# Head weights of an expert layer added up transposed in PSUM, with transposed GELUs and thresholds in place

## What is computed

```
xn = rmsnorm(x) * norm_w
q  = (xn @ w_q.T).reshape(b, t, 8 heads, 2, 128)
sim1, sim2 = q[...,0,:] . keys[...,0,:],  q[...,1,:] . keys[...,1,:]    # 32 each per head
s1, i1 = top_k(sim1, 8);  s2, i2 = top_k(sim2, 8)
fs, pk = top_k(s1[:, None] + s2[None, :], 8)          # 8 best of the 1024 experts (i, j), per head
hidden = gelu(xn . expert_down[fi]) * relu(fs)
out    = sum over heads and picks of hidden * expert_up[fi]
```

## Time and profile before

| | |
|---|---|
| median of 3 runs | 1263.45 us (1261.83 to 1265.84) |
| span of the profiled execution, the only time shown of it | 1266.5 us |
| busy, whole span: PE / DVE / ACT / POOL | 885.7 / 988.6 / 570.6 / 256.6 us |
| mean granted clock of PE | 0.839 |
| expert sublayer in the span | about 448 to 641 us, and 1060 to 1252 us |
| in it, 540 to 580 us: PE / DVE / ACT busy | 35.11 / 39.70 / 28.68 us of 40 |

### The profile page before, as it was taken

One profiled execution on the slowest core, in us unless ns is written; L12 is line 12 of the kernel. 1 busy time (PEld: TensorE's weight loads), 2 busy tenths in 40 slices (PEclk: granted clock), 3 DMA queues, 4 the chain that ended last, 5 costly groups with the idle time before them and its releaser, 6 DMA issues. The chain is left out here.

```text
span 1266.5 us, 10862 instructions
## 1 busy us (share of the span) xinstructions
PE 885.7 (70%) x3174; PEld 451.5 (36%) x3176; DVE 988.6 (78%) x1819; ACT 570.6 (45%) x1593; POOL 256.6 (20%) x125
## 2 busy tenths in 40 slices
PE   2551557767889868988826227676789996798893
PEld 1440312223346424444314112222243653344342
DVE  1278789998469579999816876999964975999993
ACT  1413353331434356865812146333333443966782
POOL 5011015554242010000000210555521501000000
PEclk9665578888989879999967568788899887999997
DMA  7100000000000000000010000000000000000000
GB/s 211 30 0 1 0 1 0 0 1 0 1 1 1 1 1 1 1 1 1 1 48 1 1 0 1 0 0 1 1 1 1 1 1 0 1 1 1 1 0 17
DMA packets 17403, 10.31 MB, mean 8 GB/s; under 512 B 6084, under 2 KB 16058, under 8 KB 17338
## 3 DMA queue, kind: packets, MB, share of 16 engines
q1 hardware_dynamic: 15368, 7.59, 2.2%
q10 hardware_dynamic: 1970, 1.97, 0.6%
HBM read 8.50 MB, written 1.05 MB: 8 GB/s over the span
## 5 line engine op out<-in xcount | busy, mean ns | idle before, releaser
L883 ACT ACTIVATE mem<-ps 77x512 f32<-77x512 f32 (+3 forms) x192 | 115.5, 603 | 387.4 <-POOL mem L1479 148.9
L1463 POOL TENSOR_TENSOR rs<-ve,minus_half 128x4 f32<-128x4 f32 (+2 forms) x60 | 102.0, 1709 | 811.5 <-DVE ve L1081 683.2
L851 PE MATMUL ps<-mem,ident 128*128 128x512 f32 x512 | 231.4, 600 | 30.5 <-DVE mem L1431 29.7
L1041 ACT ACTIVATE mem<-mem 128x32 f32<-128x32 f32 x1024 | 217.8, 308 | 0.0
L703 PE MATMUL ps<-mem,ident 128*128 128x512 f32 x256 | 154.9, 737 | 79.8 <-POOL mem L1479 79.8
L1479 POOL TENSOR_TENSOR mem<-mem 128x1024 f32<-128x1024 f32 x32 | 136.0, 4250 | 181.5 <-DVE mem L1267 181.5
L1431 DVE SCALAR_TENSOR_TENSOR mem<-mem 128x1024 f32<-128x1024 f32 x128 | 159.1, 1278 | 13.4 <-ACT mem L1041 12.0
L851 PEld LDWEIGHTS ps<-mem,ident 128*128 128x128 f32 x512 | 93.9, 190 | 167.1 <-issue 92.7
L1267 DVE TENSOR_TENSOR_SCAN mem<-mem 128x1024 f32<-128x1024 f32 x64 | 142.9, 2274 | 0.0
L1423 DVE TENSOR_TENSOR mem<-mem 128x1024 f32<-128x1024 f32 x96 | 112.9, 1216 | 0.3
L703 PEld LDWEIGHTS ps<-mem,ident 128*128 128x128 f32 x256 | 56.7, 233 | 157.1 <-POOL mem L1479 97.0
(11 more groups left out here) (223 smaller groups left out, 1269.9 us busy)
## 6 DMA issues: line engine op xcount, KB each, us to landing
x<-in_x_dram SPq DMA_DIRECT2D x4, 256.0 KB, 3.7
out_dram<-x SPq DMA_DIRECT2D x4, 256.0 KB, 2.3
mask<-in_mask_BxSxS_ik_dram SPq DMA_DIRECT2D x4, 154.0 KB, 3.5
mem<-n_L_ffn_expert_down_dram SPq DMA_DIRECT2D x1, 512.0 KB
mem<-in_L_xattn_Wo_dram SPq DMA_DIRECT2D x1, 512.0 KB
mem<-in_L_xattn_Wv_dram ACTq DMA_DIRECT2D x1, 512.0 KB
a_q<-in_L_xattn_Wq_dram SPq DMA_DIRECT2D x1, 512.0 KB, 4.4
a_k<-in_L_xattn_Wk_dram SPq DMA_DIRECT2D x1, 512.0 KB, 4.9
```

The source lines that it names most:

```text
L851: mm = pe.matmul(ps[:, j, :], ident[:], WH[s][:, h % WB, j * 512:(j + 1) * 512], start=(h == 0), stop=(h == PH - 1), skip_group_check=True)
L883: ins = nc.scalar.activation(to, of, ACT.Copy, **kw)
L1041: ins = nc.scalar.activation(SVA[s][:, n % 2, i * NK:(i + 1) * NK], sims[:, 1, h, :], ACT.Identity, bias=sims[:, 0, h, i:i + 1])
L1463: nc.gpsimd.tensor_tensor(RS[s][0:rows, i * n:(i + 1) * n], VE[s][0:rows, i * n:(i + 1) * n], minus_half[0:rows, 0:n], ALU.pow)\
```

## The change

- **PE.** WH becomes the stationary operand and the identity the moving one, in transpose mode and accumulating: for each head 8 transposes of 128 x 128 into banks 0 and 1, so that the sum over heads stands transposed (experts down the partitions, tokens along). The transposes of the product, HWT's copy and the wait for it are gone.
- **Inputs and GELUs.** The expert inputs are made transposed, one block e of 128 experts for all 512 tokens: 8 matmuls of 512 columns and 8 GELUs of 128x512 for each lane, into the new tile GT. They are slipped in between the heads of block 0: input e on PE right after head e (stages 10.6 + h and 10.65 + e), GELU e on ACT between quarters of ACT's sums. Banks 2 and 3 are a ring of two for these inputs and then the outputs (`ring_full`, `ring_free`).
- **Sums and thresholds.** Sums are written into WH, now a ring of 5, by DVE or ACT, and DVE's threshold works in place. SV and SVA are gone. ACT waits for a free slot of WH (`wh_used`), and makes its heads in quarters with the lanes by turns (stages 6.5 + 20k + h + 0.9 x quarter).
- **Order.** Block k+1's thresholds and its first sum now come ahead of block k's multiplication on DVE. The outputs of block k stand at stage 9.9 + 20(k+1) on PE and ACT, ahead of block k+1's heads on both. `merged` issues two such sequences of one lane by their numbers.
- SIM's layout is (head, half, key) instead of (half, head, key).

Core of the diff:

```diff
-    WB = 4
+    WB = 5
+        ring_order = []
+        for k in range(NB):
+            if k == 0:
+                ring_order += [(10.65 + e, "in", k, e) for e in range(EB)]
+            else:
+                ring_order += [(9.9 + 20 * k, "out", k - 1, 0)]
+        ring_order = sorted(ring_order) + [(90, "out", NB - 1, 0)]
+        RING = {entry[1:]: n for n, entry in enumerate(ring_order)}
+        def ring_bank(n):
+            return 2 + n % 2
+        def merged(*runs):
+            stage = [next(r, None) for r in runs]
+            while any(n is not None for n in stage):
+                n, i = min((n, i) for i, n in enumerate(stage) if n is not None)
+                yield n
+                stage[i] = next(runs[i], None)
 # PE
+                    def ring(*entry):
+                        n = RING[entry]
+                        if n >= 2:
+                            pe.wait_ge(G("ring_free", s), n - 1)
+                        return ring_bank(n)
+                    def expert_inputs(e):
+                        pe.matmul(ps[:, ring("in", 0, e), :], p_downT[:, e * P:(e + 1) * P], XT[s][:], start=True, stop=True)\
+                            .then_inc(G("ring_full", s), 1)
+                    def outputs(k):
+                        w.next(G("hw_ready", s))
+                        b = ring("out", k, 0)
+                        for e in range(EB):
+                            mm = pe.matmul(ps[:, b, 0:P], HWT[s][:, e, :], p_up[:, e, :],
+                                           start=(e == 0), stop=(e == EB - 1))
+                        mm.then_inc(G("ring_full", s), 1)
+                    def others():
+                        for e in range(EB):
+                            yield 10.65 + e
+                            expert_inputs(e)
+                        for k in range(NB):
+                            yield 9.9 + 20 * (k + 1)
+                            outputs(k)
+                    def weights():
+                        for k in range(NB):
+                            for h in range(PH):
+                                yield 10.6 + 20 * k + h
+                                w.next(G("wh_ready", s))
+                                if h == 0 and k >= 1:
+                                    pe.wait_ge(G("hw_ready", s), k)
+                                for e in range(EB):
+                                    mm = pe.matmul(ps[:, e // 4, (e % 4) * P:(e % 4 + 1) * P],
+                                                   WH[s][:, (k * PH + h) % WB, e * P:(e + 1) * P], ident[:],
+                                                   start=(h == 0 and e % 4 == 0), stop=(h == PH - 1 and e % 4 == 3),
+                                                   is_transpose=True, skip_group_check=True)
+                                mm.then_inc(G("wh_used", s), 1)
 # ACT
+                    def own_sums():
+                        for k in range(NB):
+                            for h in ACT_HEADS:
+                                n = k * PH + h
+                                for quarter in range(4):
+                                    yield 6.5 + 20 * k + h + 0.9 * quarter
+                                    if n >= WB and quarter == 0:
+                                        act.wait_ge(G("wh_used", s), n - WB + 1)
+                                    for i in range(quarter * NK // 4, (quarter + 1) * NK // 4):
+                                        ins = nc.scalar.activation(WH[s][:, n % WB, i * NK:(i + 1) * NK], ...)
+                                ins.then_inc(G("asum_ready", s), 1)
+                    def expert_inputs(e):
+                        of = ring("in", 0, e)
+                        nc.scalar.activation(GT[s][:, e, :], of, ACT.Gelu).then_inc(G("ring_free", s), 1)
+                    def outputs(k):
+                        of = ring("out", k, 0)
+                        copy(OS[s][:, k, :], of[:, 0:P], G("ring_free", s))
 # DVE
+                    def weighted(k):
+                        dve.wait_ge(G("wh_used", s), (k + 1) * PH)
+                        ...
+                        nc.vector.tensor_tensor(
+                            HWT[s], ps[:, 0:2, :].rearrange("p a (b c) -> p (a b) c", c=P),
+                            GT[s][:, :, k * P:(k + 1) * P], ALU.mult).then_inc(G("hw_ready", s), 1)
+                    def sums():
+                        ...
+                                    yield (17.95 + 20 * (k - 1) if h == 0 and k >= 1 else 10 + 20 * k + h)
+                                    if n >= WB:
+                                        dve.wait_ge(G("wh_used", s), n - WB + 1)
+                                    nc.vector.tensor_tensor(WH[s][:, n % WB, :]..., ALU.add)
+                    def weights():
+                        for k in range(NB):
+                            for h in range(PH):
+                                wh = WH[s][:, (k * PH + h) % WB, :]
+                                yield 10.5 + 20 * k + h
+                                ...
+                                nc.vector.scalar_tensor_tensor(
+                                    out=wh, in0=wh, scalar=TH[s][:, h:h + 1], in1=wh,
+                                    op0=ALU.is_ge, op1=ALU.mult).then_inc(G("wh_ready", s), 1)
+                            if k + 1 < NB:
+                                yield 17.9 + 20 * k
+                                best_keys(k + 1)
+                                yield 17.92 + 20 * k
+                                thresholds(k + 1)
+                            yield 18 + 20 * k
+                            weighted(k)
```

More of the change, by code:

```diff
@@ L843, in experts @@
                     yield 3
                     w.next(G("sim_sb", s), NB)
[L845 to L869, removed]
@@ L871, in _ @@
+                    yield from merged(others(), weights())
                 in_turn(sublayers([hyena, cross0, bitffn, scan, cross1, experts]))
@@ L1026, in experts, with ring @@
                         copy(SIM[s][:, k, :], ps[:, k, :], G("sim_sb", s))
[L1028 to L1043, removed]
+                    def ring(*entry):
+                        n = RING[entry]
+                        act.wait_ge(G("ring_full", s), n + 1)
+                        return ps[:, ring_bank(n), :]
@@ L1045, in experts @@
                     yield 3
                     w.next(G("sim_sb", s), NB)
[L1047 to L1051, removed]
-                        yield 18 + 20 * k
-                        w.next(G("turned", s))
-                        copy(HWT[s][:].rearrange("p (a b) c -> p a (b c)", a=2), ps[:, 2:4, :], G("hwT_ready", s))
-                        yield 19 + 20 * k
-                        w.next(G("eo_ready", s))
-                        copy(OS[s][:, k, :], ps[:, 2, 0:P], G("eo_drained", s))
-                        yield 20 + 20 * k
-                        if k + 1 < NB:
-                            activations()
+                    yield from merged(others(), own_sums())
@@ L1405, in thresholds @@
                         w.link(nc.vector.tensor_scalar(TH[s][:], TT[s][:, :, TOP - 1], 0.0, None, ALU.max))
+                    def sums():
+                        for k in range(NB):
+                            sims = SIM[s][:, k, :].rearrange("p (h a n) -> p a h n", a=2, h=PH)
+                            for h in range(PH):
+                                if h not in ACT_HEADS:
+                                    n = k * PH + h
+                                    yield (17.95 + 20 * (k - 1) if h == 0 and k >= 1 else 10 + 20 * k + h)
+                                    if n >= WB:
+                                        dve.wait_ge(G("wh_used", s), n - WB + 1)
+                                    nc.vector.tensor_tensor(
+                                        WH[s][:, n % WB, :].rearrange("p (i j) -> p i j", i=NK),
+                                        spread(sims[:, 0, h, :], 2, NK), spread(sims[:, 1, h, :], 1, NK), ALU.add)\
+                                        .then_inc(G("own_done", s), 1)
+                    def weights():
+                        for k in range(NB):
+                            for h in range(PH):
+                                wh = WH[s][:, (k * PH + h) % WB, :]
+                                yield 10.5 + 20 * k + h
+                                if h in ACT_HEADS:
+                                    w.next(G("asum_ready", s))
+                                else:
+                                    w.next(G("own_done", s))
+                                nc.vector.scalar_tensor_tensor(
[8 more added lines that the diff above has]
+                            weighted(k)
                     yield 3
@@ L1445, in experts @@
+                    yield from merged(sums(), weights())
                     yield 94
-                    w.next(G("eo_drained", s), NB)
+                    dve.wait_ge(G("ring_free", s), RING["out", NB - 1, 0] + 1)
                     residual(s, OS[s][:], None)
```

57 lines of the change are left out of this document (16 added, 41 removed).

## The result

| | before | changed |
|---|---|---|
| median | 1263.66 us (4 runs, 1261.83 to 1265.84) | 1278.76 us (4 runs, 1274.82 to 1282.59) |
| ratio | | 1.0109, 95% interval 1.008 to 1.0139 |
| span of the profiled execution | 1266.5 us | 1273.2 us (its time 1274.82, the lowest of the four) |
| busy PE / DVE / ACT / POOL | 885.7 / 988.6 / 570.6 / 256.6 | 799.7 / 988.8 / 554.2 / 256.2 |
| granted clock | 0.839 | 0.799 |

The kernel is 15 us slower; 1281.5 had been forecast (1263 to 1292). DVE does the same work in the same time, PE and ACT do less, and it is slower all the same.

A forecast was written before the change was run, and what follows sets the result against it. It took each expert block as a loop through ACT, though DVE looks like the bound. 8.5 + 2.2 - 0.2 - 1.5 = +9.0 us a pass, +18.0 for two, on 1263.45 gave 1281.5 us; range 1263 to 1292.

The forecast's parts named there:

- block 1, ACT's wait for input 0: First block: ACT queues behind GELU 0, waiting for PE's first input, so head 7 ends later; +8.5 us a pass.
- blocks 2, 3: ACT's sums start: Outputs at half clock delay ACT's sums to S+5.2 from S+4.09 (S: block's first threshold starts); +1.1 us a block.
- block 4: Fourth block of a pass: PE's clock was already at half before the change, so -0.2 us.
- tail, head 7 to lane 1's residual: End of a pass: shorter way to the residual, clock back half-way through the outputs; -1.5 us (-3.1 to +0.5).
- the signs named: First block, among others: ACT idle 5 to 8 us before the first GELU, its table load behind that wait.
- The lower bound, +6.5: First block with PE at full clock throughout: input 0 there at 471.7, so +6.5 us.
- The reason given: Blocks 2 to 4: PE idles some 8 us before the outputs, so they start at half clock.
- Threshold in place, ring of five, transposes on PE: DVE's in-place thresholds and ring waits cost 0; PE's head weights by transposes are hidden, saving nothing by themselves.
- The clock stays full: Rival: PE keeps full clock through its pauses, giving the lower bounds, 1261.6 us; chance 0.10.
- The row held against this rival: Evidence against the clock staying full: a PE pause of 2.11 us at 588.56 already cost it.
- DVE is the bound: Rival: ACT's sums come in time, 6.0 us of waits a pass go, tail gives 3.1; 1245 us, chance 0.06.
- The clock doesn't come back on transposes: Rival: PE bounds the first block at half clock, +17.7 us; 2 x 23.8 in all, 1311 us, chance 0.05.

The follow-up runs named there:

- the second set: The changed kernel again, unedited, beside a second measuring of the kernel before (1266.48 us) on another chip; 1275.13 us, ratio 1.0088.
- e1: Changed kernel with PE's expert input e issued just ahead of head e's weights instead of behind them; 1273.29 us, ratio 1.0075.
- e2: Changed kernel with block k's multiplication on DVE back ahead of block k+1's thresholds and first sum; 1265.82 us, ratio 1.0014.
- e4: Kernel before, with block k+1's thresholds moved ahead of block k's multiplication; 1292.56 us, ratio 1.0225.
- e5: Changed kernel with 3 useless matmuls more per lane on PE between head 7 and the outputs, blocks 1 to 3; 1272.24 us, ratio 1.0038.
- e7: Changed kernel with each head's eight accumulating transposes done twice in blocks 2 to 4 of a pass; 1278.39 us, ratio 1.0108.
- e3: Changed kernel with the edits of e1 and e2 together; 1251.25 us, ratio 0.9911.
- e6: e3 with PE's expert inputs one more head ahead (stage 9.55 + e); 1246.52 us, ratio 0.9856.

## Why the prediction was right

The forecast was right in sign and in cause, and the measured median, 1278.76 us, lies 2.7 us under the 1281.5 forecast. That closeness is in part luck: the two passes grew by 12.8 us where 18.0 had been summed, and the medians by 15.1 in this set and 8.7 in the second. By its steps, for a pass:

| term | predicted | measured in the profile after |
|---|---|---|
| block 1, ACT's wait for input 0 | +8.5 (6.5 to 8.8) | +6.95 (head 7 at S+36.59 for S+29.64) |
| blocks 2, 3: ACT's sums start | S+5.2, +1.1 each | S+4.52 and S+4.88, +0.5 and +0.8 |
| block 4 | -0.2 | -0.3 (head 7 at S+32.37 for S+32.66) |
| tail, head 7 to lane 1's residual | -1.5 | -1.66 (8.33 for 9.99) |
| pass | +9.0 | +6.3 |
| whole | +18.0 | +12.8 in the two passes; medians +15.1, and +8.7 in the second set |

*The first block* was over by 1.55 us. The step that was mis-sized: I put the table load behind the wait for PE and counted it on top, 1.3 us, since it stood there in the kernel before (464.07, after a wait). In the changed kernel it ran at once, at 460.38, and vanished in the wait that follows; of the signs named, this one didn't come. The twelve GELUs took some 6.1 us, not 6.6. The first of them started at S+6.56 (467.66), and PE's input had been put at S+6.43. In e1, with no wait to hide it, the load is on the way again. The lower bound, +6.5, doesn't follow from its own terms: 468.55 + 1.8 + 0.85 + 0.25 is 471.45, not 471.7, which makes it +6.3; the measured value lies above either.

*Blocks 2 and 3* were over by 0.6 and 0.3. Outputs at half clock, on the way of the loop, were forecast and came. The reason given, a pause of some 8 us, holds for block 2 alone; ahead of block 3 the clock had fallen before the pause, during sparse transposes, which the prediction didn't foresee. The clock came back some 3.9 us after PE resumed at 552.12 (a mean of 0.69 over 553.1 to 557.8 is 2.9 us at half, and 1.0 before it), where I took 4.5 from one case. In e1 ACT started at S+5.1 to 5.3 in the same place, so this term moves with the order of the moment; my 5.2 is at its upper end. The way of the loop itself, 11.80 us from head 7 to S and 27.2 us of ACT's sums, held (11.81 and 27.24). e2 and e4 shorten and lengthen it from both sides, and e5 gives the clock's share.

*Threshold in place, ring of five, transposes on PE*: 0 was put down, and where ACT sets the time 0 was measured: 1278 ns a threshold before and after, no sum's wait for a slot among the waits, and e7. Where DVE sets it there is a small gain. Blocks without a wait are 41.1 us in e2, e3 and e6 and 41.43 in block 1 of the kernel before, and the rows hold the difference: twice a block four thresholds stand in a row, which take 5.04 us before (493.10) and 4.87 in e3:

```profile
574.14 4.87 DVE L1483 SCALAR_TENSOR_TENSOR mem<-mem 128x1024 f32<-128x1024 f32 x4
```

Twice 0.17 is the 0.33 us between 41.43 and 41.10. Whether it comes from working in place or from where the operands lie is not shown.

*The rivals.* "The clock stays full": it didn't; e5 made it so for two blocks and got 42.15 us each, as the lower bound had it (43.14 - 1.0). The row held against this rival was weaker than it was taken for: at 588.56 the clock fell only at 589.5, after PE had resumed, and an equal pause of 2.12 us before 545.43 left it full. "DVE is the bound": false for this order, true for blocks 2 and 3 of e2, e3 and e6. "The clock doesn't come back on transposes": false, by the rows at e7.

What stays open: the medians over the runs differ by 15.1 us in one set and 8.7 in the other, around the 12.8 of the passes. I put this down to the clock in untouched code, whose start of the expert layer differs by up to 7.7 us among profiles (460.51 in e7, 468.22 in e5), but it is not measured run by run. Why one pause costs the clock and an equal one doesn't is open too.

## What to carry to other kernels

A busy share of 99% didn't make DVE the bound: the rest of 1.6 us a block stood at the same operation each time, and following who feeds it showed a loop through another engine. In such a loop, work that is moved ahead of a hand-over costs its full length, however full the engine is; issue first what another engine waits for, then what covers the wait (e2 got back 7.5 us a pass by this alone). A longer pause of an engine off the critical path can slow its next piece, and that piece may be on the path: in e4 the clock that PE lost in its pause cost 2 us a block.

## What the runs showed of the hardware that I had not expected

PE lost its full clock in pauses of 3.84 and 5.22 us (e4), 5.54 (the changed kernel) and 7.46 (e7), and kept it in one of 2.12 (the kernel before). Equal pauses had different ends: of two of 3.23 us in e5, one left the clock full, and behind the other it fell within 1 us of PE's resuming. Behind the pause of 7.50 us it was full again 3.9 us after PE resumed. The clock fell between pauses too: in the changed kernel, where transposes alone filled 14.2 us of 24.5, its mean was 0.82, and 1.00 in e7 with 22.5 of 24.5. Code that the experiments didn't touch began up to 7.7 us earlier or later from profile to profile, half of what this change cost. The table load ran during the wait of the GELU that needed it, where in the kernel before it stood behind such a wait. And six matmuls of no use in each of three blocks made the pass shorter (e5, 171.72 for 176.76 us).
